# Attention: inverse softmax sums laid out as rows through DRAM instead of by TensorE, fixed PSUM banks, and an earlier low part of the queries

## What is computed

```python
# x: (16, 512, 256); H = 16 heads, DQK = DV = 64
x = x + 0.5 * ffn(layernorm(x))          # slot attention, 16 experts, combine
h = layernorm(x)
q = h @ Wq + bq ; k, v = split(h @ Wkv + bkv)
q, k = rope(q), rope(k)                  # rotary embedding, per head
scores = q @ k.T / sqrt(64), masked causally
out = softmax(scores) @ v
x = x + out @ Wo + bo
x = x + 0.5 * ffn(layernorm(x))
```

## Time and profile before

| | |
|---|---|
| median of three runs | 2756.35 us (2751.7 to 2756.64) |
| the profiled execution: its own time, its span | 2756.2 us, 2754.4 us |
| PE busy over the span | 2563.0 us, 93% |
| DVE, ACT, POOL busy | 1761.7, 1621.5, 1443.1 us |
| attention, from the page's slices | about 480 to 2290 us of the span |

### The profile page before, as it was taken

The page is one execution under the profiler, slowest core; times in us unless marked ns, Lnnn a source line. Parts: engine busy times, 40 slices in busy tenths (PEclk is TensorE's granted clock), DMA queues, the critical chain, the costliest instruction groups (busy, mean ns, idle before and its releaser), DMA issues. The chain is left out here.

```text
span 2754.4 us, 52948 instructions
## 1 busy us (share of the span) xinstructions
PE 2563.0 (93%) x17368; PEld 1929.3 (70%) x17368; DVE 1761.7 (64%) x3171; ACT 1621.5 (59%) x4049; POOL 1443.1 (52%) x1264
## 2 busy tenths in 40 slices
PE   7986999899999999999999999999999997987899
PEld 5752676677777777777777777777777774753576
DVE  5741577577676776666767766677677675751476
ACT  2321443577777777677777776777777772321343
POOL 1100443767667677676776766767667661100343
PEclk9998999999999999999999999999999998998999
DMA  7459553322223222232222222322223215359543
GB/s 240 151 222 401 191 157 117 69 42 60 48 54 63 47 51 50 50 62 47 55 62 47 55 47 51 64 45 52 50 52 63 46 39 199 122 196 413 188 153 104
DMA packets 164276, 290.98 MB, mean 106 GB/s; under 512 B 38176, under 2 KB 117664, under 8 KB 159904
## 3 DMA queue, kind: packets, MB, share of 16 engines
q1 hardware_dynamic: 164000, 287.57, 36.9%
HBM read 178.43 MB, written 41.94 MB: 80 GB/s over the span
## 5 line engine op out<-in xcount | busy, mean ns | idle before, releaser
L1501 ACT ACTIVATE att_prob<-att_ps_s,att_nmax 128x512 f32<-128x512 f32 (+3 forms) x1024 | 529.9, 528 | 282.9 <-DVE att_nmax L1408 282.9
L1309 POOL TENSOR_TENSOR att_z_sb<-att_z_sb,sh_vT 128x512 f32<-128x512 f32 x255 | 330.9, 1298 | 425.8 <-DMA att_zs<-att_z_sb 425.7
L1408 DVE TENSOR_REDUCE att_nmax<-att_ps_s 128x2 f32<-128x1024 f32 (+3 forms) x512 | 410.2, 822 | 13.3
L1650 PE MATMUL att_ps_p<-sh_ident,att_prob 128*128 128x128 f32 x2560 | 395.6, 277 | 22.9 <-DVE att_probT L1420 14.5
L1431 DVE TENSOR_TENSOR att_oT_lo<-sh_kT,att_oT_hi 128x512 fp32r<-128x512 f32 x128 | 130.9, 1022 | 410.1 <-ACT att_oT_hi L1531 410.1
L1312 POOL TENSOR_TENSOR att_z_sb<-att_z_sb,att_zs 128x512 f32<-128x512 f32 x255 | 339.4, 1331 | 20.0
L1650 PEld LDWEIGHTS att_ps_p<-sh_ident,att_prob 128*128 128x128 f32 x2560 | 290.3, 140 | 74.3 <-DVE att_probT L1420 28.9
L1310 POOL TENSOR_TENSOR att_zs<-att_zs,att_sin 128x512 f32<-128x512 f32 x255 | 330.9, 1298 | 0.0
L1661 PE MATMUL att_ps_p<-att_probT,att_v_sb 128*64 128x512 f32 (+3 forms) x2048 | 306.9, 442 | 3.7 <-ACT att_probT L1526 2.4
L1661 PEld LDWEIGHTS att_ps_p<-att_probT,att_v_sb 128*64 128x64 f32 x2048 | 138.3, 137 | 176.1 <-issue 136.2
L1526 ACT COPY att_probT<-att_ps_p 128x512 f32<-128x512 f32 x384 | 216.2, 601 | 57.6 <-PE att_ps_p L1650 56.5
(11 more groups left out here) (200 smaller groups left out, 5875.5 us busy)
## 6 DMA issues: line engine op xcount, KB each, us to landing
att_zs<-att_z_sb SPq DMA_DIRECT2D x1024, 64.0 KB, 2.3
ffn_w<-in_e_W SPq DMA_DIRECT2D x56, 1024.0 KB, 13.7
ffn_wg<-in_e_Wg SPq DMA_DIRECT2D x24, 1024.0 KB, 14.6
x_normalised_transposed<-dis_b_xnT SPq DMA_DIRECT2D x32, 512.0 KB, 3.0
dis_b_x<-in_x SPq DMA_DIRECT2D x16, 512.0 KB, 4.1
ex_w<-in_e_W SPq DMA_DIRECT2D x8, 1024.0 KB, 12.9
ex_wg<-in_e_Wg SPq DMA_DIRECT2D x8, 1024.0 KB, 16.4
sh_xt<-x_normalised_transposed SPq DMA_DIRECT2D x16, 512.0 KB, 4.6
```

The costliest lines, as they stand in the source:

```text
L1309: nc.gpsimd.tensor_tensor(z[:, m, i, :], z[:, m, i, :], cos[:], ALU.mult)
L1408: nc.vector.tensor_reduce(nmax[:, p % 2, qt, :], ps[:, :, at:at + (qt + 1) * P], AX.X, ALU.max, negate=True)\
L1501: nc.scalar.activation(prob[:, p % 2, hh, PLACE[qt]], ps[:, hh, at:at + (qt + 1) * P], ACT.Exp, bias=nmax[:, p % 2, qt, hh:hh + 1], accum_ ...
L1650: last = nc.tensor.transpose(turn_bank(p, k)[:, at:at + P], prob[:, p % 2, hh, PLACE[qt]][:, kb * P:(kb + 1) * P], g.ident[:])
```

## The change

Four edits, all in `attention_phase`.

1. `spread`, `spread_sums` and `copy_r` are gone, with `rinv`. Instead SyncE writes `rsum` (now laid out head by head, 128 x 8) to a new DRAM tensor `inverse_sums` (2, 2, 512): query-major in DRAM, so that the transfer is 1024 runs of 4 bytes (`rows`), and then reads each head's row of 512 back 64 times, into 64 partitions of `R` (`spread`, two DMAs of 128 KB). In a slot p, `rows(p-1)` is the first thing on SyncE and `spread(p-1)` follows the swap of pair p+2. `divide` waits for it one slot later; `reciprocals` waits for the row write before; ScalarE's exps wait for reciprocals (`inv_s`).
2. Banks are fixed: the mix is always in bank 0, turn k in bank k%2. Turn 2 waits for `divide`; turn 1 waits for nothing new.
3. In the loading slot `query_low` stands ahead of the second half of the statistics and the moments.
4. The loads of `Wo` and the value bias share a semaphore (once, at the start).

```diff
+            def rows(j, u):
+                need_held(sp, inv_s, j, u + 1)
+                need_held(sp, spread_s, j, 32 * u)
+                sp.dma_start(r_dram[u % 2].rearrange("h (t q) -> q (h t)", t=TT), rsum[:].rearrange("p h t -> p (h t)"), allow_slow_non_contiguous=True).then_inc(row_s.sem, 16)
+
+            def spread(j, u):
+                need_held(sp, row_s, j, 16 * (u + 1))
+                need_held(sp, on_s, j, u - 1)
+                for hh in range(2):
+                    sp.dma_start(R[of_head(hh), u % 2, :], r_dram[u % 2, hh:hh + 1, :].broadcast_to([ADH, S])).then_inc(spread_s.sem, 16)
...
             def slot(t):
                 j, p = t.j, t.p
+                if t.has(p - 1):
+                    rows(j, p - 1)
                 if p == XRES:
...
                 if t.has(p + 2):
                     swap(j, p + 2)
+                if t.has(p - 1):
+                    spread(j, p - 1)
...
             def reciprocals(j, p):
                 dve.wait_ge(exp_s.sem, exp_s.at(j, 8 * p + 8))
-                need(dve, rec_s, j, p)
+                need(dve, row_s, j, 16 * p)
...
             def divide(j, p):
                 dve.wait_ge(pv_mm.sem, pv_mm.at(j, p + 1))
-                dve.wait_ge(pta_s.sem, pta_s.at(j, 4 * p + 1))
+                dve.wait_ge(spread_s.sem, spread_s.at(j, 32 * (p + 1)))
...
                     copy_pt(j, p - 1, 3)
-                if loading:
-                    statistics(j + 1, (2, 3))
-                    moments(j + 1)
                 if t.first and p == -1:
                     first_queries()
                 if t.has(p + 1):
                     query_low(j, p + 1)
+                if loading:
+                    statistics(j + 1, (2, 3))
+                    moments(j + 1)
...
-            def spread_sums(j, p):
-                pe.wait_ge(rec_s.sem, rec_s.at(j, p + 1))
-                for qt in range(TT):
-                    last = nc.tensor.transpose(turn_bank(p, 0)[:, qt * P:(qt + 1) * P], rinv[:, qt].rearrange("p h e -> p (h e)"), g.ident[:])
-                last.then_inc(pt_mm.sem, 1)
-
             def transposes(j, p, k):
-                if k == 1:
+                if k == 2:
                     need(pe, on_s, j, p)
```

More of the change, by code:

```diff
@@ L1165, in attention_phase @@
     one = lambda x: sem(n(x))
-    tab_in, bv_in, raw_in, bo_mm, bo_s, cos_s = (one(x) for x in ("tab", "bv", "raw_in", "bo_mm", "bo", "cos"))
+    tab_in, bias_in, bo_mm, bo_s, cos_s = (one(x) for x in ("tab", "out_bias_in", "bo_mm", "bo", "cos"))
     x_in, xres_in, out_s = c("x_in", 16), c("xres_in", 16), c("out", 16, 16)
@@ L1538, in slot @@
                     exps(j, p, 3)
-                if t.has(p - 1):
-                    spread(j, p - 1)
                 if t.has(p):
@@ L1792, in ffn @@
                     ffn_sems = [h for k, h in made.items() if k.startswith(("dis_", "ex_", "com_"))]
-                    attention_phase(nc, io, g, sem, x1, x2, [(sem(f"com_out{i}"), 16 * (B + 1)) for i in range(2)], ffn_sems,
+                    attention_phase(nc, io, g, sem, x1, x2, rows, [(sem(f"com_out{i}"), 16 * (B + 1)) for i in range(2)], ffn_sems,
                                     x0, xt0[:].rearrange("p c s -> p (c s)").rearrange("p (i d) -> p i d", i=TT),
```

60 lines of the change are left out of this document (24 added, 36 removed).

## The result

The changed kernel takes 3023.9 us (median of 4 runs, 3019.7 to 3024.9), against 2756.2 us for the kernel before on the same chip (2751.7 to 2756.6). The ratio is 1.097, with a 95% interval of 1.095 to 1.099. It is 268 us slower, where 60 us less were forecast. Its profiled execution has a span of 3022.6 us.

What follows compares the result with a forecast made beforehand. TensorE, 96% busy over the attention, was taken as the bound. Gains of 36.0 + 8.4 + 15.6 = 60.0 us, with nothing for DMA, took 2756.35 to 2696 us; range for 8 in 10: 2686 to 2721 us.

Steps and rivals of the forecast that it cites:

- Usual slots: Positions 0 to 3 and 7 of each batch item: removed transposes gain 0.45 us in each of 80 slots, 36.0 us.
- The slot behind the turning slot: Turn 2 no longer waits for the copy of R: 0.53 us gained in 15 slots, 8.4 us with the last.
- The row write: SyncE's write of 1024 4-byte runs to DRAM lands in about 3 us, at worst 8.4; both fit.
- Rival B: Slow 4-byte writes stand in front of the swap: slower than before, some 2870 us at 150 ns a run; chance 0.08.
- The spread: Two 128 KB reads issued behind the swap land roughly 3 us into the next slot, up to 5; nothing lost.
- Rival A: Swap late by 1.3 to 2 us because row write and spreads share its queue: 2705 to 2756 us; chance 0.12.
- SyncE's new waits: Ahead of the swap: inverses are there at 2.8 us, evacuated keys awaited at 8 us, so the wait costs nothing.
- Edit 3: Queries' low part first: loading and turning slot together gain 0.98 us, 15 times; 15.6 us with the last item.
- TensorE's wait at the third turn: In the turning slot, about 1.2 us at turn 3, 15 times, instead of waits for the queries' low part.
- Rival C: VectorE becomes the bound in usual slots too; with half of the 36.0 us given back, 2714 us; chance 0.07.
- Edit 4: Two waits of one instruction, for loads at the start, are merged; costs nothing.
- the banks: Fixed banks: turn 2 no longer waits for the copy of R, and its new wait for divide costs nothing.

Runs made afterwards that it cites:

- e1: The changed kernel without row writes and spreads, R set to one once, so the division by the sums is left out: 2763.2 us, ratio 1.002.
- e3: The changed kernel with the spreads in place but no row writes, the rows in DRAM written once at the start: 2764.4 us, ratio 1.002.
- e4: The changed kernel with the same 4 KB row write made as 128 runs of 32 bytes, rows in a wrong order: 2760.4 us, ratio 1.002.
- e9: e1 with the loading slot's statistics and moments back ahead of the queries' low part: 2733.7 us, ratio 0.991.
- e12: The changed kernel with the row write waiting for the spread of the pair two before, not just before: 2958.3 us, ratio 1.074.
- e6: The kernel before, with only the queries' low part moved ahead of statistics and moments in the loading slot: 2790.0 us, ratio 1.012.
- e10: The kernel before with one 128 x 8 transpose replacing four, rows written as 8 runs of 512 bytes, old order and banks: 2740.0 us, ratio 0.993.

## Why the prediction was wrong

**Usual slots** (36.0 us): close to right. e1 has 13.08 us against 13.46, so 0.38 a slot instead of 0.45, 30 us in 80 slots. e3, e4 and e9 agree (13.10 or 13.11). The slot behind the turning slot gained 0.43 of 0.53 us. In the changed kernel both are there and buried.

**The row write** is the step that failed, twice over. The landing was taken as about 3 us, and 8.4 was held for the worst end. It is 10.3 us in the median and up to 11.8. The nearest row was a load, and a read of 4-byte runs said nothing about writing them side by side. I held the landing only against the moment at which the spreads go out, and even there SyncE waited 205 us. What wasn't asked is who else is in flight while the write is pending. The term of the sum for that was zero, and it is 261 us. In the two slots shown the load of x was 9 us late and the swap 6 or 7.

**Rival B** had the right sign and place and nearly the right price. It let the 64 runs of each engine stand in front of the swap. The runs are taken up in 0.7 us, some 11 ns a run, so that isn't how the time goes. But from the first packet, some 0.9 us behind the issue, to completion it is about 9.4 us, or 147 ns a run, and in that time the swap and the loads hardly move. For 150 ns B gave 2870 us. (By its own rule of 128 us for each further us, 1.0 us more is 2756 + 131 = 2887.) What it left out are the loads and spreads that are late as well. Its chance of 0.08 was too little for an operation of which no row existed.

**The spread** landed in 3.2 us (forecast 2.7, at most 4.5) and cost nothing (e3). Rival A falls. That divide would wait for no DMA held in e3, not in the changed kernel (164 us).

**SyncE's new waits** were said to cost nothing. The wait of the row write for the previous spread wasn't named in the prediction at all. It closed a ring of up to 14.6 us, and loosening it took off 66 us (e12).

**Edit 3** (15.6 us with the loading slot): wrong sign. In e1 the loading slot gained 0.78 us, more than its share, and the turning slot lost 3.70, of which 2.8 go with edit 3. I had seen that VectorE was full there and that it would start about 1 us earlier, and then took its 4.87 us of normalising as fixed. That doesn't hold: they depend on where GpSimd's passes lie. TensorE's wait at the third turn was forecast as about 1.2 us and was 3.2, and the clock's drop behind it wasn't in the sum. e6 prices edit 3 alone at 30 us.

**Rival C** came true in another slot than it said: in e1 TensorE waits 76 us for copies of turns, but mostly in the turning slots. **Edit 4** and the banks show no cost of their own, but no run takes them out alone. e10 has the old banks and its usual slots take 13.15 us, e9 the new ones and 13.11.

## What to carry to other kernels

A small write that nobody waits for can still be the most expensive thing in a kernel, if everything in flight beside it is moved slowly or reported late. Ask of a DMA not only how long the engines take it up, but when it completes and what else is in flight until then, and never take a write's landing from a read. Here runs of 32 bytes side by side and runs of 4 bytes with 64 bytes from one to the next were both free; turning 128 x 8 values on TensorE costs one cheap transpose and makes the runs 512 bytes. And where two engines slow each other, an instruction's duration belongs to the schedule: moving VectorE by 1 us may change what its instructions take.

## What was not expected of the hardware

- 1024 touching 4-byte runs to DRAM, 4 KB in all: taken up in 0.7 us, complete after 8.3 to 11.8. From 64 bytes to 64 bytes 2.9 us, 512 bytes apart 2.6, as 512 touching runs of 8 bytes 3.8, as 128 of 32 bytes 1.4.
- While such a write was pending, the engines moved 29 GB/s with a load and a swap in flight. With the same load in flight they moved 182 before.
- Such a write delays transfers of another queue: a 512 KB load 14.9 us instead of 3.9, and two spreads whose data was under way within 4.1 us of the first issue were reported after 12.7 and 13.1.
- VectorE's instruction of 0.57 us takes 1.5 beside GpSimd's passes, and a shift of 1 us between the two engines moved a slot by 2.7 us.
- Around the end of each of the 15 waits of 3.2 us TensorE's clock was at half, for about 3 us or twice that. In the slot shown that costs 1.1 us more.
